# Other places for two loads and their statistics, three more warm-up products, products by half pieces, and six more pieces with `a_lo` in halves

## The reference

```python
h = maximum((x - mean(x)) / sqrt(var(x) + 1e-5), 0)     # over the 128 features of each row
out = x + 0.9 * (adj @ h) + 0.1 * L0_gnn_h
```

## Time and profile before

| what | value |
|---|---|
| median of three runs | 711.1 us |
| the profiled execution's own time | 711.17 us |
| its span, first to last instruction | 709.4 us |
| PE (TensorE matmul) busy | 703.6 us, 99% |
| PEld (weight loads) busy | 577.5 us, 81% |
| DVE (VectorE) busy | 627.1 us, 88% |
| ACT (ScalarE) busy | 524.4 us, 74% |
| POOL (GpSimd) busy | 39.7 us, 6% |
| DMA | 285.73 MB, mean 403 GB/s |
| granted TensorE clock | 0.999 |

### The profile page before, as it was taken

The page is one execution under the profiler, slowest core; times in us unless marked ns, Lnnn a source line. Parts: engine busy times, 40 slices in busy tenths (PEclk is TensorE's granted clock), DMA queues, the critical chain, the costliest instruction groups (busy, mean ns, idle before and its releaser), DMA issues.

```text
span 709.4 us, 7934 instructions
## 1 busy us (share of the span) xinstructions
PE 703.6 (99%) x3079; PEld 577.5 (81%) x3079; DVE 627.1 (88%) x474; ACT 524.4 (74%) x356; POOL 39.7 (6%) x23
## 2 busy tenths in 40 slices
PE   8999999999999999999999999999999999999998
PEld 4878888888888888888888888888888888888886
DVE  5889999999999989999898888888988898889885
ACT  5888787888777878788767677776767676767673
POOL 1001111011010111010000000000000000000000
PEclk9999999999999999999999999999999999999999
DMA  9999999999999999999999999999999999999990
GB/s 353 409 408 412 421 419 417 423 417 418 421 419 420 421 419 420 419 419 422 414 401 413 394 396 396 404 385 405 419 421 421 421 420 423 420 420 422 404 418 18
DMA packets 47557, 285.73 MB, mean 403 GB/s; under 512 B 5280, under 2 KB 5792, under 8 KB 17824
## 3 DMA queue, kind: packets, MB, share of 16 engines
q1 hardware_dynamic: 47232, 284.77, 98.2%
q10 hardware_dynamic: 288, 0.46, 0.2%
HBM read 281.02 MB, written 4.19 MB: 402 GB/s over the span
## 4 chain that ended last, share of the span: by engine, by line
PE 94%; DMA 3%; DVE 1%; SPq 1%; ACT 1%; issue 0%; DVEq 0%
PE acc L443 16%; PE acc L438 16%; PE acc L439 16%; PE acc L427 15%; PE acc L422 15%; PE acc L416 15%; DMA raw<-early_dram 3%; DVE a_lo L328 1%; SPq L206 1%; ACT a_hi L284 0%; ACT h_full L251 0%; DVE finished L347 0%; SPq L191 0%; DVEq L119 0%; DVEq L346 0%
## 5 line engine op out<-in xcount | busy, mean ns | idle before, releaser
L328 DVE TENSOR_TENSOR a_lo<-raw,a_hi 128x2048 fp32r<-128x2048 f32 (+1 forms) x262 | 581.4, 2225 | 59.4 <-ACT a_hi L284 58.6
L284 ACT ACTIVATE a_hi<-raw 128x2048 fp32r<-128x2048 f32 (+1 forms) x276 | 491.4, 1782 | 169.4 <-PE acc L443 100.1
L438 PE MATMUL acc<-a_hi,h_hi 128*128 128x512 f32 x512 | 199.2, 389 | 0.0
L439 PE MATMUL acc<-a_hi,h_lo 128*128 128x512 f32 x512 | 199.2, 389 | 0.0
L443 PE MATMUL acc<-a_lo,h_hi 128*128 128x512 f32 x512 | 136.8, 389 | 0.0
L427 PE MATMUL acc<-a_lo,h_hi 128*128 128x512 f32 x504 | 135.1, 390 | 0.2 <-DVE a_lo L328 0.2
L416 PE MATMUL acc<-a_hi,h_hi 128*128 128x512 f32 x504 | 135.2, 390 | 0.0
L422 PE MATMUL acc<-a_hi,h_lo 128*128 128x512 f32 x504 | 134.7, 389 | 0.0
L438 PEld LDWEIGHTS acc<-a_hi,h_hi 128*128 128x128 f32 x512 | 96.1, 188 | 20.0
L443 PEld LDWEIGHTS acc<-a_lo,h_hi 128*128 128x128 f32 x512 | 96.1, 188 | 20.0
L439 PEld LDWEIGHTS acc<-a_hi,h_lo 128*128 128x128 f32 x512 | 96.1, 188 | 19.9
(11 more groups left out here) (15 smaller groups left out, 29.4 us busy)
## 6 DMA issues: line engine op xcount, KB each, us to landing
raw<-tall_dram SPq DMA_DIRECT2D x128, 1024.0 KB, 8.0
raw<-wide_dram SPq DMA_DIRECT2D x104, 1024.0 KB, 11.1
raw<-early_dram SPq DMA_DIRECT2D x48, 512.0 KB, 11.7
res_sb<-res_dram SPq DMA_DIRECT2D x16, 512.0 KB, 9.8
out_dram<-finished SPq DMA_DIRECT2D x15, 256.0 KB, 8.2
x_sb<-x_dram SPq DMA_DIRECT2D x14, 256.0 KB, 11.5
x_sb<-x_dram ACTq DMA_DIRECT2D x1, 256.0 KB, 4.6
out_dram<-finished SPq DMA_DIRECT2D x2, 128.0 KB, 1.8
```

Of the source, the lines that this page charges most:

```text
L284: nc.scalar.activation(a_hi[:, q % SPLIT_SLOTS, cols], raw[:, q % RAW_SLOTS, cols], ACT.Copy).then_inc(hi_ready, 1)
L328: nc.vector.tensor_tensor(a_lo[:, q % SPLIT_SLOTS, cols], raw[:, q % RAW_SLOTS, cols], a_hi[:, q % SPLIT_SLOTS, cols].bitcast(fp32), ALU.s ...
L438: nc.tensor.matmul(bank, h_hi[:, k, :], a_hi[:, slot, cols], start=(k == 0), stop=False)
L439: nc.tensor.matmul(bank, h_lo[:, k, :], a_hi[:, slot, cols], start=False, stop=False)
```

## The change

Six edits, all at the start of the program:

1. 18 warm-up products in place of 15.
2. The load of `x` of blocks 4 to 7 (unit 1) is no longer issued by ScalarE at the start but by SyncE behind the loads of piece 1. The load for blocks 8 to 11 (unit 2) moves from behind piece 4 to behind piece 8.
3. VectorE makes `h_lo` of unit 0 ahead of the statistics of unit 1, and the shift of unit 1 after `low_a` of piece 2.
4. The statistics of unit 2 are taken two blocks after `low_a(9)` and two after `low_a(10)`; its aggregate comes after `low_a(11)` and its shift after `low_a(12)`. `scale_unit`, `high_h` and `low_h` of unit 2 stay at 12, 13, 14 and 15.
5. In wide pieces the products with `a_hi` go by half pieces: two of `h_hi`, two of `h_lo`, then the same for the second half.
6. `a_lo` is made in halves for pieces 2 to 15, not 2 to 9.

```diff
-EARLY, EARLY_LOW = 24, 10
+EARLY, EARLY_LOW = 24, 16
...
-LOAD_X_AT = {}
-STATS_AT, AGGREGATE_AT, SHIFT_AT = {}, {}, {}
-SCALE_AT, HIGH_H_AT, LOW_H_AT = {3: (1, 0), 4: (1, 1)}, {5: 1}, {6: 1}
-for _u in range(2, UNITS):
+LOAD_X_AT = {NATIVE: 1, 9: 2}
+STATS_AT, AGGREGATE_AT, SHIFT_AT = {9: [8, 9], 10: [10, 11]}, {11: 3}, {NATIVE: 2, 12: 3}
+SCALE_AT, HIGH_H_AT, LOW_H_AT = {3: (1, 0), 4: (1, 1), 12: (2, 0), 13: (2, 1)}, {5: 1, 14: 2}, {6: 1, 15: 2}
+for _u in range(3, UNITS):
...
-WARM_UP = 15
+WARM_UP = 18
...
-            act.dma_start(x_sb[:, UNIT:2 * UNIT, :], x[:, UNIT:2 * UNIT, :]).then_inc(x_landed[2], 16)
...
             make_shift(1)
+            low_h(0)
             for k in range(UNIT, 2 * UNIT):
...
             aggregate(2)
-            make_shift(2)
-            low_h(0)
...
+                for half in (range(0, QUAD // 2), range(QUAD // 2, QUAD)):
+                    for j in half:
+                        cols = slice(j * SEG, (j + 1) * SEG)
+                        pe.wait_ge(hi_ready, split_through(q, part_of(q, j)))
+                        nc.tensor.matmul(acc[:, quad * QUAD + j, :], h_hi[:, k, :], a_hi[:, slot, cols],
+                                         start=False, stop=False)
+                    if fresh and half.start == 0:
+                        pe.wait_ge(h_lo_ready, k // UNIT + 1)
+                    for j in half:
...
+                        nc.tensor.matmul(acc[:, quad * QUAD + j, :], h_lo[:, k, :], a_hi[:, slot, cols],
+                                         start=False, stop=False)
```

## The result

The changed kernel takes 712.42 us, the median of 22 runs (711.47 to 713.41), against 711.08 (710.75 to 712.30) for the kernel before in as many. The ratio is 1.0018 with a 95% interval of 1.0012 to 1.0024: 1.3 us slower, and the sign is certain: the interval is 0.4 us to each side, narrower than the 1.4 us that the forecast thought a measurement can tell. That is inside the forecast's range and under its line of 0.2%, but it is 0.8 us more than the 0.5 that the sum gave. The profiled execution took 712.31 us, 1.14 more than the one of before.

The account below looks back on a forecast made before the run. TensorE's products bound the kernel from piece 20, VectorE close behind. The product needing a_lo of piece 19 moves from 63.04 to 63.5, +0.5: 711.6 us against the 711.1 median, range 710.1 to 712.6.

Parts of the forecast that it names:

- its line of 0.2%: What a measurement of this kernel can tell from no change: about 0.2%, 1.4 us; same means 709.7 to 712.5.
- What bounds the kernel: TensorE's products run without loss from piece 20 (64.03 us); the change can only move that start, tenth for tenth.
- VectorE's row of work to the late shift: VectorE from piece 9's second half (33.25) works 9.27 us without pause; unit 2's shift starts at 42.52, ScalarE waits 1.9.
- VectorE from there: From 47.23, 13.93 us of VectorE work; a_lo of piece 19 starts at 61.16 instead of 60.65.
- GpSimd: Unit 2's rstd slips in between two VectorE instructions at piece 12 and is done at 42.33, before the shift.
- The rival that has it held off by both halves: GpSimd's rstd waits for both a_lo halves of piece 12, until 43.5: +1.0, 712.6 us; chance 0.12.
- the start: Edits 1, 2, 5: first real product at about 5.15 without a gap, piece 2 ends at 15.07 against 16.98.
- the rest of edits 2 and 3: Unit 1's x lands by 9.6, its shift is done by 14.6; no cost, under 0.5 us each if uncovered.
- The gap at piece 9: Piece 9's data stay 1.44 us late, likely from an instruction-queue packet; halves land at 30.87 and 32.15, lead falls to 0.9.
- The rival with a smaller gap: The gap at piece 9 is smaller or absent, so VectorE's row starts earlier: 710.2 us; chance 0.17.
- The lead of 1.9: TensorE ends piece 2 1.9 us earlier; 0.9 left after piece 9, none by piece 13; not in the sum.

Follow-up runs that it names:

- the kernel with the later scale: Changed kernel with both scale halves and h_hi of unit 2 one piece later (13, 14, 15): 711.94 us against 711.16 for the kernel before, ratio 1.0012.
- one repair: Changed kernel with the load of x for blocks 4 to 7 issued by ScalarE at the start again: 711.44 us against 711.16 before, ratio 1.0003.
- both repairs: Changed kernel with x of blocks 4 to 7 issued by ScalarE, and unit 2's scale halves and h_hi one piece later: 711.06 us against 711.01 before.
- the kernel above: Kernel before with 18 warm-ups in place of 15 and nothing else: 711.04 us against 711.14, ratio 0.9999.

## Why the prediction was right, and where its size was not

- **What bounds the kernel** held: all of the +1.17 stands at the start of piece 20, and nothing comes after it.
- **VectorE's row of work to the late shift** held term by term: from the second half of piece 9 to the shift 9.27 us were forecast (33.25 to 42.52); in the trace it starts behind the copy done at 33.93 and reaches 43.19, so 9.26. Edit 4 alone and its repair show that this row, by ScalarE's wait, is a cause. Its worth in the changed kernel is the 0.6 between it (+1.3) and the kernel with the later scale (+0.8), or the 0.2 between the kernels with one repair (+0.3) and with both (+0.05).
- **VectorE from there** held: 13.93 forecast from 47.23 to 61.16; in the trace 47.91 to 61.80, 13.89.
- **GpSimd** held: `rstd` ended at 43.00, 0.87 after the first half of piece 12 (40.91 + 1.22) and beside the second, and the pair of halves took its normal 2.36. The rival that has it held off by both halves is out. The slower time that it named, 712.6, was nearly met by another mechanism.
- **The failed step is the start.** The forecast said that the first product "no longer waits for the 256 KB that left the front of the queue", and of piece 9 that "as many bytes are ahead as before, so its halves still land at 30.87 and 32.15". Of the rest of edits 2 and 3 it said that they "otherwise cost nothing". It counted bytes at a constant rate, and the load had also left a queue of its own. From 4 to 7 us the rate fell from 402 to 247 GB/s, the first half of piece 2 landed 2.2 us later instead of level, `x` of unit 1 landed at 11.7 and not by 9.6, and the 0.7 to 0.8 that was left of the delay at piece 9 went through VectorE's row of work to the end: 0.5 + 0.65 is nearly the 1.17 of the trace. The experiments put the term at +1.35 alone and at 1.0 within the change (712.42 against 711.44).
- **The gap at piece 9 was wrong too, and the other way.** The forecast kept 1.44 us of it; in the changed kernel 0.13 is left. Had both delays stood in full, piece 9 would have come 1.3 later and the time would be about 713.7 (an estimate from these rows), outside the forecast's range. That the time fell inside it is in part luck: two errors of opposite sign met. The rival with a smaller gap had the gap right, but not the start, and its 710.2 was missed.
- **How the two delays met** is in the trace's records of landings. Each load has sixteen, and the load is in with the last. Before, they lie 0.5 us apart from first to last up to piece 8, and 1.9 from piece 9 on; in the changed kernel 2.0 from piece 2 on, and 1.9 to 2.1 at piece 9. So one delay mostly hides behind the other and doesn't add to it. All thirteen traces agree: in the nine where piece 2 is copied within 0.3 us of 10.85 the gap at piece 9 is 1.1 to 1.7 us (in one of them half a piece earlier), in the four where piece 2 comes 0.8 to 2.2 late it is 0.1 to 0.9. In all of them a 16 KB packet of the instruction queue lies just ahead of that gap, at 27.2 to 29.7 us, and takes 1.0 to 1.1 us. That it makes the gap stays likely; no run moved it.
- **The lead of 1.9** never came about, since the data for it weren't there; the forecast had spent it by piece 13 anyway, so this error costs the sum nothing. Two kernels show that an earlier start is worth nothing here: the one with both repairs starts piece 3 at 15.50 and took 711.06, the one with edits 1, 5 and 6 alone starts it at 17.50 and took 710.95.
- The Trainium skill, "DMA: Bandwidth & Descriptors", section "Issuing engines are not separate DMA queues", says that loads issued by several engines interleave on the same DMA engines and that this only saves issue time. The traces disagree from 4 to 7 us (247 to 313 GB/s against 388 to 410), and the measurement decides. In the steady stretch no run here had loads on two queues, so there nothing is shown either way.

## What to carry to other kernels

Where a chain of waits enters the bounding engine late, find the first place from which that engine never waits again, and price a change only by what it does to that place; a lead ahead of it is worth nothing. When work is bunched on the engine that runs close behind the bound, look for the instruction of a third engine that waits for the bunch's last result and for what is queued behind it. And a transfer that is moved from one queue to another moves two things, its bytes and its queue: at the start of this program the second was the larger. Lastly, two delays of loads on one queue need not add up: of 2.1 and 1.4 us together only 2.3 were left here.

## What was not expected of the hardware

- From 4 to 7 us one queue alone moved 0.74 MB, against 1.21 MB with a second one (0.20 MB of them its own). From 7 to 10 us the kernel before has one queue alone as well, and moves 423 GB/s. Why some packets are slow at the start only isn't settled.
- The number of warm-ups didn't decide when TensorE's clock rose. With 15, the passes were at 0.86 us to 8.4 in one execution and at 0.43 from 6.22 on in another; with 18, at 0.43 from 6.96 on in the changed kernel and at 0.86 to 9.4 in the kernel above. The profile's column for the granted clock reads 1.00 from 4 to 10 us in all of them, so the level is read from the time of the passes. The row of the kernel with edit 6 alone, 15 warm-ups:

```profile
6.22 0.19 PEld L405 LDWEIGHTS acc<-raw,h_full 128*128 128x128 f32 x1 [0.24 <-issue]
```

- GpSimd can be first too. In the kernel with edit 4 alone `rstd` began while VectorE was free, and VectorE's next `a_lo` waited 0.32 for it without a named releaser:

```profile
41.14 1.01 POOL L244 TENSOR_TENSOR rstd<-var_eps,exponent 128x4 f32<-128x4 f32 x1 [31.21 <-DVE var_eps L307]
41.38 2.29 DVE L328 TENSOR_TENSOR a_lo<-raw,a_hi 128x2048 fp32r<-128x2048 f32 x1 [0.32 <-issue]
```
